# The attention middle section: two products moved from GpSimd to VectorE, and the inverse norms copied out of PSUM by ScalarE

## The reference

```
q  = (layernorm(x) @ W_q.T)  split into 16 heads of 128;  kv likewise
qf  = fft(q, axis=-1);   kvf = fft(kv, axis=-1)
qf  = qf / norm(qf);     kvf = kvf / norm(kvf)      # over the 128 of a head
kvf = cumsum(kvf, axis=sequence)
values = real(ifft(qf * kvf));   attention = values @ W_o.T
x = x + layernorm(attention);    then the feed-forward block
```

## Time and profile before

| | us |
|---|---|
| median of 3 runs (lowest, highest) | 1716.42 (1713.99, 1717.37) |
| the profiled execution, device time | 1716.55 |
| its span on the slowest core, core 2 | 1714.7 |
| spans of the eight cores | 1700.9 to 1714.7 |
| busy in the span: PE, DVE, ACT, POOL | 1306.3, 749.5, 386.5, 212.1 |

### The profile page before, as it was taken

The page is one execution under the profiler, slowest core; times in us unless marked ns, Lnnn a source line. Parts: engine busy times, 40 slices in busy tenths (PEclk is TensorE's granted clock), DMA queues, the critical chain, the costliest instruction groups (busy, mean ns, idle before and its releaser), DMA issues. The chain is left out here.

```text
span 1714.7 us, 15704 instructions; the slowest of 8 cores (1700.9 to 1714.7 us)
## 1 busy us (share of the span) xinstructions
PE 1306.3 (76%) x5920; PEld 543.1 (32%) x5920; DVE 749.5 (44%) x945; ACT 386.5 (23%) x378; POOL 212.1 (12%) x187
## 2 busy tenths in 40 slices
PE   3489999979999955655656615999973888888885
PEld 2334444424444411111111101444432444443442
DVE  4500000000000049999999930444442554555453
ACT  3410111011101134444444400000002233233321
POOL 1100000000000003333333340111110000000000
PEclk9999999989999966666666556999996988988887
DMA  6521221122122100000000049455442112221221
GB/s 105 96 42 33 37 37 26 24 37 37 27 36 37 25 2 0 0 0 0 0 0 1 0 66 155 100 121 111 111 106 67 61 51 74 74 71 41 74 74 49
DMA packets 21921, 86.21 MB, mean 50 GB/s; under 512 B 3008, under 2 KB 3144, under 8 KB 19800
## 3 DMA queue, kind: packets, MB, share of 16 engines
q0 software_dynamic: 21232, 84.98, 23.2%
q1 hardware_dynamic: 616, 0.23, 0.1%
HBM read 111.46 MB, written 25.17 MB: 80 GB/s over the span
## 5 line engine op out<-in xcount | busy, mean ns | idle before, releaser
L306 PE MATMUL PMAIN<-AR,OV 128*128 128x512 bf16 x2048 | 457.9, 382 | 38.8 <-ACT AR L332 13.6
L306 PEld LDWEIGHTS PMAIN<-AR,OV 128*128 128x128 bf16 x2048 | 197.5, 98 | 299.6 <-issue 75.8
L345 DVE TENSOR_TENSOR OV<-AR 128x2048 bf16<-128x2048 bf16 x32 | 39.2, 1226 | 492.7 <-ACT AR L335 492.7
L849 PE MATMUL PAUX<-AR 128*128 128x512 bf16 x1024 | 235.6, 393 | 0.0
L410 ACT ACTIVATE AR<-PAUX 128x1024 bf16<-128x1024 f32 x128 | 127.0, 1022 | 169.6 <-PE PAUX L453 108.4
L573 PE MATMUL PMAIN<-AR 128*128 128x512 bf16 x512 | 121.4, 400 | 40.5 <-DMA AR<-wot 40.5
L849 PEld LDWEIGHTS PAUX<-AR 128*128 128x128 bf16 x1024 | 101.7, 101 | 126.3 <-issue 15.9
L332 ACT ACTIVATE AR<-PMAIN 128x1024 bf16<-128x1024 f32 x32 | 32.7, 1023 | 414.6 <-PE PMAIN L306 414.6
L453 PE MATMUL PAUX<-AR,MSIN 128*128 128x512 bf16 x128 | 61.1, 590 | 68.6 <-ACT AR L410 67.4
L573 PE MATMUL PAUX<-AR 128*128 128x512 bf16 x512 | 111.8, 379 | 0.0
L469 POOL TENSOR_TENSOR AR<-AR 128x2048 bf16<-128x2048 bf16 x16 | 65.8, 4114 | 287.1 <-DVE AR L484 287.1
(11 more groups left out here) (114 smaller groups left out, 1172.0 us busy)
## 6 DMA issues: line engine op xcount, KB each, us to landing
AR<-x POOLq DMA_DIRECT2D x32, 512.0 KB, 5.4
out<-AR POOLq DMA_DIRECT2D x16, 1024.0 KB, 5.1
OV<-wqs POOLq DMA_DIRECT2D x16, 512.0 KB, 5.0
OV<-wkvs POOLq DMA_DIRECT2D x16, 512.0 KB, 5.0
AR<-wot POOLq DMA_DIRECT2D x16, 512.0 KB, 27.5
x1s<-AR POOLq DMA_DIRECT2D x16, 512.0 KB, 3.0
AR<-wt POOLq DMA_DIRECT2D x16, 512.0 KB, 7.0
AR<-x1s POOLq DMA_DIRECT2D x16, 512.0 KB, 5.9
```

The lines of the kernel that those rows point to most:

```text
L306: ins = te.matmul(PMAIN[:, nn * 512:(nn + 1) * 512], lhsT, XCT[:, c * 2048 + nn * 512: c * 2048 + (nn + 1) * 512], start=(c == 0), stop=(c ...
L345: v.tensor_mul(SQ[h % 2], DEST[:, h * 2048:(h + 1) * 2048], DEST[:, h * 2048:(h + 1) * 2048]).then_inc(s_sq, 1)
L849: te.matmul(PAUX[:, nn * 512:(nn + 1) * 512], lhsT, WTB[:, c * 2048 + nn * 512: c * 2048 + (nn + 1) * 512], start=(c == 0), stop=False)
```

## The change

The diff, whole:

```diff
+    INVB = [OV1[:, 4096:5120], OV1[:, 5120:6144],
+            AR2[:, 14336:15360], AR2[:, 15360:16384]]
+    s_qkm = sm("s_qkm")
 # scalar engine, b2
-                for j in range(4, 12):
+                for j in range(12):
                     p = j % 2
                     a.wait_ge(s_dft, 12 * h + j + 1)
+                    if j < 4:
+                        if h >= 1:
+                            a.wait_ge(s_qkm, 4 * (h - 1) + j + 1)
+                        a.activation(INVB[j],
+                                     PAUX[:, p * 1024:(p + 1) * 1024],
+                                     AF.Identity).then_inc(sf[p], 1)
+                        continue
                     if j == 4 and h >= 1:
                         a.wait_ge(s_scand, h)
                     if j == 8 and h >= 1:
                         a.wait_ge(s_cm, h)
-                        a.wait_ge(s_gprod, h)
 # tensor engine, b2
+                    if j in (4, 5):
+                        te.wait_ge(s_qkm, 4 * h + 3 + (j - 4))
+                    if j in (8, 9):
+                        te.wait_ge(s_qkm, 4 * h + 1 + (j - 8))
 # gpsimd, b2: its whole program of 16 heads goes
-                g.tensor_tensor(T1G, QF_RE, KVC_RE, ALU.mult)
-                g.tensor_tensor(T2G, QF_IM, KVC_IM, ALU.mult
-                                ).then_inc(s_gprod, 1)
 # vector engine, b2
             def midsec_a(v, h):
-                if h >= 1:
-                    v.wait_ge(s_gprod, h)
             def midsec_b(v, h):
+                v.tensor_mul(T1, QF_RE, KVC_RE)
+                v.tensor_mul(T2, QF_IM, KVC_IM)
+                v.drain()
+                v.wait_ge(s_ifft, h)
+                v.tensor_sub(QV_RE, T1, T2)
+                v.drain()
                 v.tensor_mul(T1, QF_RE, KVC_IM)
                 v.tensor_mul(T2, QF_IM, KVC_RE)
                 v.drain()
-                v.wait_ge(s_ifft, h)
-                v.tensor_add(QV_IM, T1, T2)
-                v.drain()
-                v.wait_ge(s_gprod, h + 1)
-                v.tensor_sub(QV_RE, T1G, T2G).then_inc(s_cm, 1)
+                v.tensor_add(QV_IM, T1, T2).then_inc(s_cm, 1)
                 v.drain()
 # vector engine, the four multiplications by the inverse norms
-                    v.wait_ge(s_dft, 12 * h + j + 1)
+                    v.wait_ge(sf[p], 6 * h + j // 2 + 1)
-                                 PAUX[:, p * 1024:(p + 1) * 1024]
-                                 ).then_inc(sf[p], 1)
+                                 INVB[j]).then_inc(s_qkm, 1)
```

## The result

| | before | changed |
|---|---|---|
| median, us | 1716.34 (10 runs) | 1688.74 (9 runs) |
| ratio, 95% interval | | 0.9842 [0.9831, 0.9852] |
| profiled execution, device time | 1716.55 | 1685.98 |
| stage b2, each of the eight cores | 377.3 to 377.6 | 342.1 to 342.4 |
| stage d, mean of the cores | 432.1 | 438.9 |

A forecast was written before the change was run, and what follows sets the result against it. VectorE was taken to bound stage b2, at 22.39 us a head. Gains of 2.9 at the start, 23.5 over fourteen rounds and 5.4 at the end sum to 31.8: 1716.55 - 31.8 = 1684.8 us, range 1665 to 1705.

The forecast's parts named there:

- B: VectorE's last piece of a b2 round, from M's end: six SBUF instructions, 7.60 us against 8.43 before.
- the 4.56: Duration in us of B's first product before, against 1.21 for the second; claimed to be a hold by GpSimd's product.
- M: VectorE's four 128 x 1024 multiplications between scans and B; 0.65 us each with SBUF inputs, against 1.21 with PSUM.
- The rival that the copy buys nothing: M's instructions stay at 1.21 us despite SBUF inputs; round 21.71, time 1701 us; chance 0.13.
- That rival's late case: The same with VH's copy late: round 22.16 us, time 1707 us.
- The new wait: M waits for ScalarE's four inverse copies behind VH's copy and the back transform; this path sets a 20.71 us round.
- four stations: After B's end: VH's copy starts +6.3, fourth inverse copy ends 12.39, 0.15 crossing to M's last, 0.57 to first product.
- Start, rounds, end: Stage b2's gains: 2.9 us to the first end of B, 23.5 over fourteen rounds, 5.4 in the last round.
- the first one: Barriers close each stage, so every microsecond gained or lost in b2 passes to the kernel's end in full.
- The rival that the copies are free: Inverse copies are ready when the scans end, so VectorE's 19.08 us is the round; time 1662 us; chance 0.10.
- The loop was no longer: Rival: engine crossings cost double, M stays at 1.21 and VH is late, giving no change; chance 0.05.

The follow-up runs named there:

- e1: Kernel before with only the products moved: all four multiplications on VectorE, M still reading the inverse norms in PSUM; 1703.16 us, ratio 0.9916.
- e2: Changed kernel with the real part's two products back on GpSimd, so only the inverse copies remain; 1754.16 us, ratio 1.0213 to the kernel before.
- e3: Changed kernel with the next head's four inverse half tiles made and copied ahead of the back transform and VH's copy; 1671.67 us, ratio 0.9733.
- e4: Kernel before with 17 drains added to VectorE's program at the start of stage b1q; 1725.01 us, ratio 1.0036.
- e6: Changed kernel with 111 drains on VectorE and 192 already fulfilled waits on TensorE, restoring both code places; 1681.77 us, ratio 0.9794 to the kernel before.
- e9: Kernel before with 128 drains added to VectorE's program at the start of stage b1q; 1717.93 us, ratio 1.0002.
- e10: Kernel before with 64 already fulfilled waits added to TensorE's program in ph1; 1723.23 us, ratio 1.0025.

## Why the prediction was right, and where not

- *B.* Six instructions, no hold: 7.60 forecast, 7.46 measured; two of the steps behind a drain take 1.30 and 1.29 where I took 1.37 and 1.36 from before. The cause of the 4.56 is shown by e1 and e2.
- *M.* 0.69 where I took 0.65, in a range of 0.61 to 1.21. Almost no effect, since VectorE waits in M anyway: only the last one's 0.61 until the first product, for 0.57, is on the path. The rival that the copy buys nothing was wrong on the duration, yet right in part of the sense: in the changed kernel the wait eats most of what M's speed gives. Products alone give 20.5 of b2's 35.2 (e1), the copies the other 14.7; with the order of e3 they give another 20. That rival's late case is summed 0.1 a round too long: its third copy ends at +11.92, so M ends at 14.45 and not 14.56, the round is 22.05 and the time 1706.
- *The new wait.* The path, with its four stations, holds to 0.13 us at each, as listed above; of the 0.23 between 20.48 and 20.71, 0.14 are B's and 0.09 the stations'. That the start of VH was so near, 6.27 for 6.3, is in part luck: it was picked between 5.67 and 6.75, which would have given 20.08 and 21.16, and no row told that the changed kernel would settle there.
- *Start, rounds, end.* B first ended 663.45 - 630.18 = 33.3 after the stage's barrier work, before 35.8: 2.5 (forecast 2.9). Fourteen rounds to 948.82 + 1.23 = 950.05 gave 27.0 (23.5; the term that was 3.5 too small, by 0.23 to 0.25 a round). The last round took 16.66 (16.80), 5.5 gained (5.4):

```profile
948.82 1.23 DVE L499 TENSOR_TENSOR AR<-AR 128x2048 bf16<-128x2048 bf16 x1
...
959.25 1.23 DVE L490 TENSOR_TENSOR AR<-AR 128x2048 bf16<-128x2048 bf16 x1 [0.23 <-issue]
...
965.48 1.23 DVE L499 TENSOR_TENSOR AR<-AR 128x2048 bf16<-128x2048 bf16 x1
```

- *The step that failed* is the first one: "I let every microsecond gained or lost here pass to the end in full". It was named at the end of the prediction as a way to be wrong, but priced at nothing. Stage d did not keep its length: 6.8 us longer, by where in a round code is fetched (e4, e6, e9, e10, and the count over all loads). This outweighs the 3.5 that the rounds gave beyond the forecast: 1684.8 forecast, 1688.7 measured. Either error alone would have stayed inside the range of 1665 to 1705 (1681 and 1692); that the median lies within 4 of the forecast owes something to their opposite signs.
- The rival that the copies are free fell for the changed kernel (VectorE waits in M) and is the state of e3. The loop was no longer than the rows showed. One reading of the slices was off by one and bears on nothing: VectorE is busy 90% or more from the 16th to the 23rd; the 15th, in which b2 starts, has 4 tenths.

What stays open: why one fetch delays the load by 0.5 to 1.6 us, half of the time by under 0.9, with 8 KB among 1.5 MB, and why not every fetch does: in one round of e1, of e3 and of the changed kernel q14 moves at +3.0, beside 24 loads in all, of which none landed after +7.1. A single DMA engine's share arriving last would fit, and was not tried. Nor was the place varied to find the best; before happened to have no late load at all.

## What to carry to other kernels

When work is moved off an engine onto one that runs ahead of the bound, follow the in-order queue of the receiving engine from release to release: the copies cost nothing by ScalarE's busy share and still set the round, because they stood behind a wait. Before giving an engine a second SBUF operand, look what GpSimd reads at that time. And when a stage that nobody touched changes by one or two per cent, look at the `instruction` queues and at a period in rounds before blaming the clock.

## What the runs showed of the hardware that was not expected

- VectorE with two SBUF inputs and a GpSimd product of SBUF tiles take turns whole: 0.69 becomes about 4.5 (e2), 1.22 becomes 4.56 to 5.07. With one operand in PSUM there is no hold (4.84 for four beside GpSimd).
- The place of code: 17 more instructions on VectorE cost 4.4 us in a later stage, 64 on TensorE 4.8, 128 on VectorE nothing; where VectorE's place was moved, it stands about 0.35 us at the same line in every second round, and with either place moved many loads that have a fetch beside them land later (at most +7.0 becomes +7.5 to +8.6, half of them within +7.8). The Trainium skill (Runtime: NRT & Kernel Launch, Instruction fetch mechanics) says that code streams in blocks of 16 KB through a DMA queue and that the cost of crossing a block is mostly hidden. The traces show the streaming, in packets of 16 KB on TensorE's queue as the page has it, but of 8 KB on VectorE's; and the cost was not hidden here: 6.8 of 1689 us. On both the measurement decides.
